# A gated recurrent block with a ternary feed-forward layer: loads spread over two queues, small steps moved between engines

## The reference, cut to what matters

```
xn = (x - mean) / sqrt(var + 1e-5)
y  = gelu(xn @ w_y + b_y);   xb = xn @ w_x + b_x
conv[t] = conv_b + sum_k conv_w[k] * xb[t - 3 + k]            # 4 taps
gate_x = sigmoid(conv @ w_ig + b_ig);  gate_a = sigmoid(conv @ w_ag + b_ag)
a = exp(-8 * gate_a * softplus(a_param)); mult = sqrt(1 - a*a)
h[t] = a[t] * h[t-1] + gate_x * conv * mult                   # scan over t
out = x + (h * y) @ w_out + b_out
        + ((silu(xn @ w1q.T) * (xn @ w3q.T)) @ w2q.T)         # w1q, w3q, w2q: rounded to -s, 0, s
```

## Time and profile before

| | |
|---|---|
| profiled execution | 72.7 us, of which the span of the instructions is 70.9 us |
| median of three runs | 72.7 us |
| PE busy | 67.0 us, 95% of the span |
| DVE busy | 56.5 us, 80% |
| ACT busy | 52.1 us, 73% |
| POOL busy | 42.4 us, 60% |
| moved by DMA | 6.66 MB, nearly all of the input in the first 18 us |

### The profile page before, as it was taken

One profiled execution on the slowest core, in us unless ns is written; L12 is line 12 of the kernel. 1 busy time (PEld: TensorE's weight loads), 2 busy tenths in 40 slices (PEclk: granted clock), 3 DMA queues, 4 the chain that ended last, 5 costly groups with the idle time before them and its releaser, 6 DMA issues.

```text
span 70.9 us, 1026 instructions
## 1 busy us (share of the span) xinstructions
PE 67.0 (95%) x327; PEld 56.2 (79%) x327; DVE 56.5 (80%) x100; ACT 52.1 (73%) x80; POOL 42.4 (60%) x57
## 2 busy tenths in 40 slices
PE   4999999999999999999999999999999999999940
PEld 4998898877888888888888888888888889987630
DVE  0098898999999999999939964198976999996660
ACT  3395798599989999999989768989969961333000
POOL 6577874799996591000000899678796698566300
PEclk9999999999999999999999999999999999999999
DMA  0899999999000000000000000000000000000564
GB/s 0 293 226 320 393 400 404 389 340 359 18 0 0 5 0 0 0 0 0 0 5 0 5 0 9 0 0 0 0 0 0 0 0 0 0 0 0 191 246 155
DMA packets 4021, 6.66 MB, mean 94 GB/s; under 512 B 476, under 2 KB 1456, under 8 KB 4016
## 3 DMA queue, kind: packets, MB, share of 16 engines
q1 hardware_dynamic: 3728, 6.46, 25.6%
q10 hardware_dynamic: 288, 0.14, 0.7%
HBM read 5.56 MB, written 1.05 MB: 93 GB/s over the span
## 4 chain that ended last, share of the span: by engine, by line
PE 66%; DVE 10%; POOL 5%; issue 5%; ACT 4%; DMA 4%; POOLq 2%; DVEq 0%
PE slot L790 26%; PE slot L773 24%; DVE slot L668 5%; PE slot L853 4%; PE slot L886 4%; DMA par<-params 4%; PE slot L821 3%; PE slot L799 3%; PE slot L762 2%; POOL rstd L271 2%; DVE slot L657 2%; POOLq L52 2%; POOL conv_lo L347 2%; ACT L462 2%; DVE tx L674 1%
## 5 line engine op out<-in xcount | busy, mean ns | idle before, releaser
L301 POOL TENSOR_TENSOR g_lo<-w_raw,g_hi 128x512 fp32r<-128x512 f32 x10 | 12.9, 1303 | 14.6 <-DVE tx L641 12.3
L790 PE MATMUL slot<-xt_hi,w_q 128*128 128x512 f32 x40 | 15.7, 393 | 0.0
L790 PE MATMUL slot<-xt_lo,w_q 128*128 128x512 f32 x40 | 15.7, 393 | 0.0
L629 DVE SCALAR_TENSOR_TENSOR w_raw<-w_raw,s,slot 128x512 f32<-128x512 f32 x10 | 7.4, 747 | 4.9 <-ACT w_raw L407 4.9
L607 DVE SCALAR_TENSOR_TENSOR conv<-slot,par,conv 128x511 f32<-128x511 f32 (+2 forms) x12 | 9.0, 748 | 0.4
L790 PEld LDWEIGHTS slot<-xt_lo,w_q 128*128 128x128 f32 x40 | 7.5, 188 | 1.7
L790 PEld LDWEIGHTS slot<-xt_hi,w_q 128*128 128x128 f32 x40 | 7.5, 188 | 1.7
L407 ACT ACTIVATE w_raw<-slot,scale 128x512 f32<-128x512 f32 x10 | 6.8, 689 | 2.4 <-PE slot L790 2.3
L811 PE MATMUL slot<-g_hi,w_q 128*128 128x512 f32 (+1 forms) x25 | 8.3, 346 | 0.0
L811 PE MATMUL slot<-g_lo,w_q 128*128 128x512 f32 (+1 forms) x25 | 8.2, 346 | 0.0
L293 POOL TENSOR_TENSOR conv_lo<-conv,conv_hi 128x512 fp32r<-128x512 f32 x4 | 5.9, 1473 | 1.5 <-ACT conv_hi L428 1.4
(11 more groups left out here) (127 smaller groups left out, 164.8 us busy)
## 6 DMA issues: line engine op xcount, KB each, us to landing
w_raw<-w13t SPq DMA_DIRECT2D x2, 682.0 KB, 7.4
w_raw<-dense SPq DMA_DIRECT2D x5, 256.0 KB, 5.5
x_both<-x SPq DMA_DIRECT2D x4, 256.0 KB, 4.0
x_both<-xt SPq DMA_DIRECT2D x2, 512.0 KB, 5.3
out<-x_both SPq DMA_DIRECT2D x3, 256.0 KB, 2.1
w_raw<-w2t SPq DMA_DIRECT2D x1, 640.0 KB
out<-x_both ACTq DMA_DIRECT2D x1, 128.0 KB, 2.0
out<-x_both SPq DMA_DIRECT2D x1, 128.0 KB, 1.7
```

Source lines behind the costliest of these rows:

```text
L301: nc.gpsimd.tensor_tensor(g_lo[:, j, s], g[:, n % RING], g_hi[:, j, s].bitcast(f32), ALU.subtract).then_inc(g_lo_set, 1)
L629: nc.vector.scalar_tensor_tensor(out=g[:, n % RING], in0=silu[:, n % RING], scalar=s32[:, 0:1], in1=slot[H_SLOT[s][j]][:, 1], op0=ALU.mult ...
L790: mm = nc.tensor.matmul(slot[H_SLOT[s][j]][:, o], w13_q[:, c, col:col + P], v[:, s, c], start=(c == 0 and v is xt_hi), stop=(c == KC - 1 a ...
```

## The change

- `WARM` goes from 12 to 11.
- Loads. SP brings tile 0 of sequence 0 alone (128 KB), then tiles 2 and 3, then both halves of sequence 1, w_y and so on. ACT's queue brings tile 1 (128 KB), then w_x, then `par`.
- Before it waits for `par`, ACT runs one more activation, an Ln of one column of zeros whose result nobody reads.
- POOL: the `gt` memset moves into the opening; the tap products move behind both powers of sequence 0, and the four sums behind the low part of w_x.
- The last `hy_lo`, (1,1), moves from POOL to DVE, between the first and second `output`; PE makes the two pieces of sequence 0 one after the other.

```diff
-WARM = 12
+WARM = 11
-            for i in range(2):
-                tiles_of_x(0, i)
-            square(WX)
-            for i in range(2):
-                tiles_of_x(1, i)
+            sp.dma_start(x_sb[:, 0, 0], x[0][:, 0]).then_inc(x_loaded[0], 16)
+            sp.dma_start(x_sb[:, 0, 2:TILES], x[0][:, 2:TILES]).then_inc(x_loaded[2], 16)
+            for i in range(2):
+                t = slice(i * TILES // 2, (i + 1) * TILES // 2)
+                sp.dma_start(x_sb[:, 1, t], x[1][:, t]).then_inc(x_loaded[3 + i], 16)
...
+            nc.gpsimd.memset(gt[96:P].bitcast(f32), 0.0).then_inc(gt_pads_set, 1)
+            pool.wait_ge(gt_pads_set, 2)
...
+            rstd_of(0, slice(0, TILES // 2), 1)
+            rstd_of(0, slice(TILES // 2, TILES), 2)
             tap_biases()
-            rstd_of(0, slice(0, TILES // 2), 1)
-            tap_sum(0)
-            rstd_of(0, slice(TILES // 2, TILES), 2)
-            for i in range(1, TAPS):
-                tap_sum(i)
             pool.wait_ge(xn_set, TILES)
             square_lo(WX)
+            for i in range(TAPS):
+                tap_sum(i)
...
         def _(act):
+            act.dma_start(x_sb[:, 0, 1], x[0][:, 1]).then_inc(x_loaded[1], 16)
+            act.dma_start(w_raw[:, WX], dense[WX]).then_inc(w_loaded[WX], 16)
             act.dma_start(par[:, :], params).then_inc(par_loaded, 16)
+            act.wait_ge(quarter_set, 2)
+            nc.scalar.activation(gelu_in[:, 1:2], gelu_in[:, 0:1], ACT.Ln, bias=1.0)
...
             for i in range(2):
-                dve.wait_ge(x_loaded[i], 16)
-                statistics(0, tile_halves[i])
+                for t in tile_halves[i]:
+                    dve.wait_ge(x_loaded[min(t, 2)], 16)
+                    statistics(0, [t])
                 variance(0, tile_halves[i])
...
-            for n in range(len(O_ALL)):
+            output(0)
+            last_hy_lo()
+            for n in range(1, len(O_ALL)):
                 output(n)
...
-            project(0, range(len(O_PARTS[0])))
-            for i in range(len(O_PARTS[1])):
-                project(1, [i])
+            for s in range(SEQS):
+                for i in range(len(O_PARTS[s])):
+                    project(s, [i])
```

More of the change, by code:

```diff
@@ L142, in xt_bank @@
             return slot[T_SLOT[s]][:, h].rearrange("p (c n) -> p c n", c=KC)
-        x_loaded = [sem(f"x_loaded{i}") for i in range(2 * SEQS)]
+        x_loaded = [sem(f"x_loaded{i}") for i in range(2 * SEQS + 1)]
         w_loaded = [sem(f"w_loaded{m}") for m in range(5)]
@@ L182, in build @@
             sem("t_psum"), sem("silu_t_set"), sem("g_t_set"), sem("gt_hi_set"), sem("gt_lo_set"))
-        hy_hi_set, hy_lo_set = sem("hy_hi_set"), sem("hy_lo_set")
+        hy_hi_set, hy_lo_set, hy_lo_last_set = sem("hy_hi_set"), sem("hy_lo_set"), sem("hy_lo_last_set")
         o_psum, o_set = sem("o_psum"), sem("o_set")
@@ L202, in square @@
                 sp.dma_start(w_raw[:, m], dense[m]).then_inc(w_loaded[m], 16)
-            def tiles_of_x(s, i):
+            sp.dma_start(x_sb[:, 0, 0], x[0][:, 0]).then_inc(x_loaded[0], 16)
+            sp.dma_start(x_sb[:, 0, 2:TILES], x[0][:, 2:TILES]).then_inc(x_loaded[2], 16)
+            for i in range(2):
                 t = slice(i * TILES // 2, (i + 1) * TILES // 2)
-                sp.dma_start(x_sb[:, s, t], x[s][:, t]).then_inc(x_loaded[2 * s + i], 16)
-            for i in range(2):
-                tiles_of_x(0, i)
-            square(WX)
-            for i in range(2):
-                tiles_of_x(1, i)
+                sp.dma_start(x_sb[:, 1, t], x[1][:, t]).then_inc(x_loaded[3 + i], 16)
             square(WY)
@@ L319, in _ @@
             lo_of_conv(0, 0)
-            pool.wait_ge(conv_lo_set, 1)
-            nc.gpsimd.memset(gt[96:P].bitcast(f32), 0.0).then_inc(gt_pads_set, 1)
-            pool.wait_ge(gt_pads_set, 2)
             lo_of_conv(0, 1)
@@ L343, in _ @@
                 gated_products(c)
[L344 to L347, removed]
+            for n in range(SEQS * KC - 1):
+                s, c = divmod(n, KC)
+                pool.wait_ge(hy_hi_set, n + 1)
+                nc.gpsimd.tensor_tensor(hy_lo[:, s, c], tx[:, s, c], hy_hi[:, s, c].bitcast(f32), ALU.subtract).then_inc(hy_lo_set, 1)
         @block.scalar
         def _(act):
+            act.dma_start(x_sb[:, 0, 1], x[0][:, 1]).then_inc(x_loaded[1], 16)
+            act.dma_start(w_raw[:, WX], dense[WX]).then_inc(w_loaded[WX], 16)
             act.dma_start(par[:, :], params).then_inc(par_loaded, 16)
+            act.wait_ge(quarter_set, 2)
+            nc.scalar.activation(gelu_in[:, 1:2], gelu_in[:, 0:1], ACT.Ln, bias=1.0)
             def square_hi(m):
@@ L674, in gated_output, with last_hy_lo @@
                 nc.vector.tensor_tensor(tx[:, s, c], state(s, c), y[:, s, c], ALU.mult).then_inc(hy_set, 1)
+            def last_hy_lo():
+                s, c = SEQS - 1, KC - 1
+                dve.wait_ge(hy_hi_set, SEQS * KC)
+                nc.vector.tensor_tensor(hy_lo[:, s, c], tx[:, s, c], hy_hi[:, s, c].bitcast(f32), ALU.subtract).then_inc(hy_lo_last_set, 1)
             def output(n):
@@ L707, in _ @@
             xt_lo_of(0, [0])
-            dve.wait_ge(x_loaded[2], 16)
+            dve.wait_ge(x_loaded[3], 16)
             statistics(1, [0])
@@ L712, in _ @@
             variance(1, tile_halves[0])
-            dve.wait_ge(x_loaded[3], 16)
+            dve.wait_ge(x_loaded[4], 16)
             statistics(1, tile_halves[1])
@@ L817, in project @@
                     for k, (v, w, ready) in enumerate(((hy_hi, w_hi, hy_hi_set), (hy_hi, w_lo, hy_hi_set), (hy_lo, w_hi, hy_lo_set))):
-                        pe.wait_ge(ready, KC * s + c + 1)
+                        if v is hy_lo and KC * s + c + 1 == SEQS * KC:
+                            pe.wait_ge(hy_lo_last_set, 1)
+                        else:
+                            pe.wait_ge(ready, KC * s + c + 1)
                         for i in banks:
```

## The result

The changed kernel took 77.31 us, the median of 4 runs (76.9 to 77.69); the kernel before took 72.75 in its 4. The ratio is 1.0612, with a 95% interval of 1.0581 to 1.0644: 4.5 us slower. The forecast was slower, 75.6 us, with a range of 73.0 to 76.7, so the direction was right and the time lies 0.6 us above the range. The profiled execution took 76.9 us with a span of 75.1, 4.2 more than before.

What follows compares the result with a forecast made beforehand. TensorE was taken to bound the kernel, through its first w_x product and the end. Later first product +2.2, clock +1.1 and end -0.35 gave +2.95 on 72.7: 75.6 us, range 73.0 to 76.7.

Steps and rivals of the forecast that it cites:

- Bound: Whole kernel: TensorE is busy 95% of the span, so each microsecond its first w_x product starts later is one at the end.
- Table loads: ScalarE, opening: three loads instead of one shared table, two behind the vectors' landing; w_x's copy 3.24 us after it.
- Landing of the vectors: Opening, ScalarE's queue: the vectors, issued third, land at 5.2 us, between bounds of 4.3 and 6.3.
- P + 4.56 - 7.58: TensorE's first w_x product: starts 4.56 us after the vectors land at P, against 7.58 before; +2.2 at P = 5.2.
- Clock: TensorE, opening: a hole of some 2.5 us between transposes and products lowers the clock; +1.1 taken.
- its own bound of 2.6: TensorE, opening: upper cost of the lower clock, 5.1 us at half speed, 2.6 us of lost work.
- Tiles 2 and 3: Opening loads of x: sharing with w_x, they land at 4.9 us, 0.4 after VectorE wants them.
- Tap sums: GpSimd, before sequence 1's power: four sums delay its transposes by 0.38 us, not added if TensorE is later anyway.
- End: After the scans: the last low part on VectorE removes TensorE's wait and slower restart; -0.35 us.
- WARM at 11 and the gt memset: Opening: warm products end 0.43 us sooner, and the memset fits GpSimd's idle time; price 0 each.
- +2.2: TensorE's first w_x product: at 9.76 us instead of 7.58; +1.3 to +3.3 over the landing's range.

Runs made afterwards that it cites:

- the one-table run: The changed kernel with its extra Ln replaced by an explicit load of the set natural_log_exp_and_others; ratio 1.0045 against the kernel before, median 73.47 us.
- With SyncE silent: The changed kernel with the named-set load instead of the extra Ln, and SyncE waiting for the vectors before issuing sequence 1 and all that follows; ratio 1.0092.
- the extra Ln alone: The kernel before with only an Ln added on ScalarE ahead of its wait for the vectors; ratio 1.0024, 0.17 us.
- the tap sums alone: The kernel before with only the tap products and the four sums moved as in the change; ratio 1.0054, 0.39 us slower.
- the end alone: The kernel before with only the last hy_lo on VectorE between the outputs and sequence 0's two pieces made one after the other; ratio 0.9965, 0.25 us faster.
- after: The changed kernel with the whole change, as profiled; median 77.31 us, profiled at 76.9, ratio 1.0612 against the kernel before.

## Why the prediction was right in its mechanism and short in its size

- **Bound (right).** The later start of TensorE's first product came out at the end in full: +3.09, +1.49 and -0.41 make the 4.17 by which the last output came later.
- **Table loads (right).** Three loads, the copy of w_x 3.16 us behind the vectors (forecast 3.24), and the one-table run shows that this is what decided. No trace names the table sets; the traces show which instruction had a load ahead of it.
- **Landing of the vectors (the step that failed).** The prediction counted "The bytes ahead of them, 768 KB over both queues", had 5.7 from them and took 5.2 us, between its lower end and 6.3. It was 6.27. The formula for the first product, P + 4.56 - 7.58, gives +3.25 with this P against +3.09 measured, so the landing is more than the whole error of this term. What the count left out is what SyncE sends beside the vectors, the halves of sequence 1 and the weights, issued from 1.63 on. With SyncE silent they landed at 5.14, near the 5.2 that was taken (by luck, since it was a middle between two bounds); with it busy at 6.2 to 6.8. The prediction had read in the earlier trace rows that the two queues are served by turns, used it for x and w_x, and not for the 128 small packets behind them.
- **Clock (mis-sized, and what put the time above the range).** "I take +1.1" stood for 1.49 in the profiled run. In two of the four runs the mean clock was lower again (0.955 against 0.977) and the time 0.6 to 0.8 us longer. The upper end of the range, 76.7, had the landing almost as it came (6.3), but paired it with the middle value of the clock and not with its own bound of 2.6, which would have made it 78.2.
- **Tiles 2 and 3 (right, and hidden).** Forecast 4.9, landed 4.9.
- **Tap sums (right in direction, size in part by luck).** +0.38 forecast alone, 0.39 measured alone (0.23 to 0.55), but the step behind the figure, transposes that finish 0.38 later, measured 0.22 to 0.24 in the chains where the sums show; where the rest comes from is open. They lie inside the larger delay in the change, as said. What the prediction did not see is their other side: the products' old place would have been far worse with late vectors.
- **End (right).** -0.35 forecast; -0.41 in the profiles, -0.25 (0.11 to 0.39) by the ratio of the part alone.
- **WARM at 11 and the gt memset.** Each priced at 0. No run varied either alone, so they stay untested.

By terms, +2.2 was +3.09, +1.1 was +1.49, -0.35 was -0.41: 1.2 us more than forecast in the profiled run. The median is another 0.4 up, by the two runs with the lower clock.

## What to carry to other kernels

Before moving a small transfer back in a queue, list every engine that waits for it and what stands behind that wait: here ScalarE's table loads and GpSimd's powers both did. In this kernel an Ln put first brought a table load more and not fewer, so rather than rely on an ordering trick, name the set, and count the table loads in the trace. A delay at the start of a TensorE-bound kernel can cost more than itself once it leaves TensorE idle, here 1.49 us on top of 3.09; when two unknown costs come from one delay, their upper ends belong together in the range.

## What the runs showed of the hardware that was not expected

- A transfer of 11 KB behind two larger ones on its queue took 4.6 to 5.2 us to land in five profiles while the other queue was busy, and 3.5 in one with it silent. Placed first it took 2.8 to 2.9.
- The same load of w_x, same issue time (1.63 us) and order, landed 3.5, 4.3, 4.6 and 5.3 us after issue in four profiles (the extra Ln alone, the tap sums alone, before, the end alone).
- After 2.4 us of idleness TensorE's clock fell only when work had begun again: granted 1.00 through the hole and for 0.7 us of products, then 0.50 from 11.4 to 14.8 us. With a hole of 1.2 us it stayed at 1.00 in the profiled execution; two other executions of the same kernel, without a trace, had a mean of 0.977.
- At the start, the warm products and transposes of 128 columns change from 0.21 us apart to 0.11 at about 4.6 us in after and in the end alone, at 6.2 in before and at 6.9 in the tap sums alone. The granted clock reads 1.00 there throughout, so it can't be taken at its word before that change.
- Back to back, a table load cost 1.29 to 1.30 us from its start to the next instruction's (6.51 to 7.81, 8.03 to 9.32), with no further wait behind it.
